# Linear attention: another order of instructions on TensorE, VectorE and ScalarE, both function-table loads moved, and the query's positive part taken by ScalarE

## The reference

```python
x = x + 0.5 * _L0_ffn_ref(_layernorm(x), ...)      # routed attention
x = x + _L0_attn_ref(_layernorm(x), ...)           # causal softmax attention
x = x + 0.5 * _L0_ffn_ref(_layernorm(x), ...)
x = x + 0.5 * _L1_ffn_ref(_layernorm(x), ...)      # 8 experts, top 2
x = x + _L1_attn_ref(_layernorm(x), ...)           # this one
x = x + 0.5 * _L1_ffn_ref(_layernorm(x), ...)

def _L1_attn_ref(x, Wq, Wk, Wv, Wp, bp, conv_w, conv_b):
    q, k, v = split_heads(x @ Wq.T), split_heads(x @ Wk.T), split_heads(x @ Wv.T)   # 16 heads of 8
    q = jax.nn.elu(q) + 1.0
    k = jax.nn.elu(k) + 1.0
    kv_state = jnp.einsum('bhnd,bhne->bhde', k, v)
    k_state = k.sum(axis=2)
    attn_out = jnp.einsum('bhnd,bhde->bhne', q, kv_state)
    denom = jnp.maximum(jnp.einsum('bhnd,bhd->bhn', q, k_state), 1e-06)[..., None]
    attn_out = (attn_out / denom).transpose(0, 2, 1, 3).reshape(b, s, d)
    xp = jnp.pad(x, ((0, 0), (1, 1), (0, 0)))
    local = xp[:, :-2, :] * conv_w[:, 0] + xp[:, 1:-1, :] * conv_w[:, 1] + xp[:, 2:, :] * conv_w[:, 2] + conv_b
    return (attn_out + local) @ Wp.T + bp
```

## Time and profile before

| | |
|---|---|
| median of 3 runs | 766.7 us (765.39 to 770.39) |
| profiled execution | 768.21 us |
| its span, first to last instruction | 766.4 us |
| PE busy | 614.0 us (80%) |
| DVE busy | 448.3 us (59%) |
| ACT busy | 426.9 us (56%) |
| POOL busy | 306.1 us (40%) |
| chain that ended last | PE 50%, ACT 18%, DVE 17%, issue 8%, DMA 4%, POOL 3% |
| mean granted TensorE clock | 0.913 |

### The profile page before, as it was taken

One profiled execution on the slowest core, in us unless ns is written; L12 is line 12 of the kernel. 1 busy time (PEld: TensorE's weight loads), 2 busy tenths in 40 slices (PEclk: granted clock), 3 DMA queues, 4 the chain that ended last, 5 costly groups with the idle time before them and its releaser, 6 DMA issues.

```text
span 766.4 us, 13125 instructions
## 1 busy us (share of the span) xinstructions
PE 614.0 (80%) x4624; PEld 454.7 (59%) x4624; DVE 448.3 (59%) x1401; ACT 426.9 (56%) x806; POOL 306.1 (40%) x384
## 2 busy tenths in 40 slices
PE   6789886379999997079887599999559769999990
PEld 3667683122222223067687589999547658999990
DVE  7883959831123215984858555556469783555572
ACT  5664634579999997444635543434343563434440
POOL 1243443213232321234341567766340036777553
PEclk9789999759999999589998799999879968999995
DMA  8311000668200000002002686666220057666645
GB/s 325 122 66 48 1 2 0 206 197 288 83 2 1 1 2 1 0 16 98 2 2 48 178 264 225 187 221 192 94 68 0 2 145 274 183 224 188 214 125 171
DMA packets 36051, 85.60 MB, mean 112 GB/s; under 512 B 5072, under 2 KB 20048, under 8 KB 34960
## 3 DMA queue, kind: packets, MB, share of 16 engines
q1 hardware_dynamic: 30992, 74.42, 29.5%
q0 software_dynamic: 4992, 10.31, 4.7%
HBM read 67.90 MB, written 16.81 MB: 111 GB/s over the span
## 4 chain that ended last, share of the span: by engine, by line
PE 50%; ACT 18%; DVE 17%; issue 8%; DMA 4%; POOL 3%; SPq 0%; ACTq 0%; DVEq 0%; POOLq 0%
PE ps L2021 17%; ACT arena L1494 9%; PE ps L2033 8%; PE ps L1725 3%; PE ps L1821 2%; ACT Xn L1302 2%; PE ps L1934 2%; PE ps L1767 1%; PE ps L1776 1%; PE ps L1800 1%; DVE stats L666 1%; DMA arena<-in_wq 1%; PE ps L1911 1%; DMA arena<-yd 1%; PE ps L2008 1%
## 5 line engine op out<-in xcount | busy, mean ns | idle before, releaser
L2021 PE MATMUL ps<-arena 128*128 128x256 f32 (+1 forms) x736 | 147.2, 350 | 2.9 <-issue 1.3
L1547 ACT ACTIVATE arena<-ps,arena 128x256 f32<-128x256 f32 (+1 forms) x184 | 81.0, 441 | 122.0 <-issue 76.6
L1494 ACT ACTIVATE arena<-ps 128x1024 f32<-128x1024 f32 x144 | 132.5, 1339 | 2.2 <-PE ps L1911 1.8
L2021 PEld LDWEIGHTS ps<-arena 128*128 128x128 f32 x736 | 122.2, 191 | 17.9 <-issue 3.4
L1018 DVE SCALAR_TENSOR_TENSOR arena<-ps,arena 128x256 f32<-128x256 f32 (+1 forms) x184 | 81.4, 443 | 75.6 <-ACT arena L1547 73.8
L639 POOL DMA_INDIRECT yd<-arena,wqk x78 | 76.7, 983 | 60.4 <-DVE arena L1040 49.4
L603 POOL DMA_INDIRECT arena<-xs,wqk x78 | 75.7, 970 | 37.6 <-issue 14.6
L590 POOL TENSOR_SCALAR_AFFINE_SELECT arena<-arena 128x512 f32<-128x512 f32 x64 | 39.9, 636 | 106.3 <-ACT arena L1494 106.3
L1934 PE MATMUL ps<-arena 128*32 128x512 f32 (+3 forms) x768 | 79.5, 502 | 1.0
L2033 PE MATMUL ps<-arena 128*128 128x128 f32 x624 | 77.3, 276 | 0.0
L2033 PEld LDWEIGHTS ps<-arena 128*128 128x128 f32 x624 | 73.3, 192 | 0.4
(11 more groups left out here) (298 smaller groups left out, 1138.3 us busy)
## 6 DMA issues: line engine op xcount, KB each, us to landing
arena<-in_wall SPq DMA_DIRECT2D x46, 836.0 KB, 4.6
arena<-slots SPq DMA_DIRECT2D x2, 2048.0 KB, 7.8
arena<-scr_q SPq DMA_DIRECT2D x8, 512.0 KB, 6.6
arena<-scr_k SPq DMA_DIRECT2D x8, 512.0 KB, 7.7
arena<-yd SPq DMA_DIRECT2D x8, 512.0 KB, 5.5
xs<-Xn SPq DMA_DIRECT2D x8, 260.0 KB, 5.5
scr_q<-arena SPq DMA_DIRECT2D x4, 384.0 KB, 4.5
scr_k<-arena SPq DMA_DIRECT2D x4, 384.0 KB, 4.2
```

What stands on the lines that cost most here:

```text
L1494: nc.scalar.activation(Pa[:, n0:n0 + FILL, :], ps[:, bank:bank + FILL, :], ACT.Exp, scale=AD ** -0.5).then_inc(sem("exp", i), 1)
L1547: nc.scalar.activation(sl[:, k % 3, 0:rows], ps[:, k % 3, 0:rows], ACT.Silu, bias=raw[:, slot, EW_BA + f:EW_BA + f + 1]).then_inc(sem("sil ...
L2021: ins = mm(ps[:, bank, 0:rows], raw[:, slot, w + P * f:w + P * (f + 1)], xTt[:, j % 2, 0:rows], start=True, stop=True)
```

## The change

Five things are done:

- **ScalarE, tables.** The dummy activation that loads the table of exp moves from behind `transposed(2)` to behind the roots of the second batch, ahead of its normalised rows. A second one, for the square root, is added behind the query activations; the next step's own dummy activation for the square root then finds its table loaded. The number of table loads stays.
- **ScalarE, queries.** Beside exp of a query chunk ScalarE now also takes its positive part, into the two slots of r2, and signals `qexp` after that. It waits for `lk(3)` and `lk(4)` before the first two (r2 is shared with the keys), and for `lq(1)` and `lq(2)` before the others.
- **VectorE, queries.** `query_map` is one scalar_tensor_tensor on SBUF tiles, in place of a tensor_scalar and a scalar_tensor_tensor that reads PSUM.
- **VectorE, order.** `local(0)` stands ahead of the first `key_map`; `local(1)` behind the second one; two query maps stand ahead of the KV masks, two behind.
- **TensorE, order.** Two query chunks go ahead of the fourth key chunk. The convolution's products (`convolved`) no longer stand together behind `state`, but one by one between the query products, transposes and projections.

The diff, cut to its core:

```diff
-                key_map(0)
-                local(0)
-                key_map(1)
-                key_map(2)
-                local(1)
-                key_map(3)
-                for c in range(NC):
+                def query_map(c):
                     dve.wait_ge(*at("qexp", i, c + 1))
                     sl_ = slice(HALF * c, HALF * (c + 1))
-                    link(nc.vector.tensor_scalar(lE[:, sl_], lE[:, sl_], 1.0, None, ALU.min))
-                    nc.vector.scalar_tensor_tensor(out=lqT[:, sl_], in0=ps[:, c, :], scalar=0.0, in1=lE[:, sl_],
-                                                   op0=ALU.max, op1=ALU.add).then_inc(sem("lq", i), 1)
-
+                    nc.vector.scalar_tensor_tensor(out=lqT[:, sl_], in0=lE[:, sl_], scalar=1.0,
+                                                   in1=r2_[:, c % 2].rearrange("p t d -> p (t d)"), op0=ALU.min, op1=ALU.add
+                                                   ).then_inc(sem("lq", i), 1)
+
+                local(0)
+                key_map(0)
+                key_map(1)
+                local(1)
+                key_map(2)
+                key_map(3)
+                query_map(0)
+                query_map(1)
                 for b in range(B):
                     dve.wait_ge(*at("state", i, b + 1))
...
+                query_map(2)
+                query_map(3)
...
                 def normal_batch(b):
                     roots(i, b)
+                    if b == B - 1:
+                        preload(ACT.Exp)
                     act.wait_ge(*at("offset", i, b + 1))
...
                 transposed(i, 2)
-                preload(ACT.Exp)
                 keys_values(0)
...
                     act.wait_ge(*at("lqp", i, c + 1))
-                    nc.scalar.activation(lE[:, HALF * c:HALF * (c + 1)], ps[:, c, :], ACT.Exp
+                    nc.scalar.activation(lE[:, HALF * c:HALF * (c + 1)], ps[:, c, :], ACT.Exp)
+                    if c < 2:
+                        act.wait_ge(*at("lk", i, c + 3))
+                    else:
+                        act.wait_ge(*at("lq", i, c - 1))
+                    nc.scalar.activation(r2_[:, c % 2].rearrange("p t d -> p (t d)"), ps[:, c, :], ACT.Relu
                                          ).then_inc(sem("qexp", i), 1)
+                preload(ACT.Sqrt)
...
+                transpose_chunk(i, 0)
+                for c in range(3):
+                    transpose_chunk(i, c + 1)
+                    key_value(c)
+                query(0)
+                query(1)
+                key_value(3)
+                query(2)
+                query(3)
+                pe.wait_ge(*at("ones_bias", i, 1))
+                pe.wait_ge(*at("krelu", i, NC))
+                state(0)
+                state(1)
+                attended(0)
+                attended(1)
+                convolved(0)
+                turned_back(0)
+                convolved(1)
+                turned_back(1)
+                attended(2)
+                projected(0)
+                attended(3)
+                projected(1)
+                turned_back(2)
+                convolved(2)
+                turned_back(3)
+                projected(2)
+                convolved(3)
+                projected(3)
```

More of the change, by code:

```diff
@@ L2050, in lin, with key_value, query, state @@
                 pe.wait_ge(sem("smallw_in"), 48)
[L2051 to L2058, removed]
+                def key_value(c):
+                    pe.wait_ge(*at("xT", i, c + 1))
+                    if c >= 2:
+                        pe.wait_ge(*at("krelu", i, c - 1))
                     for t in range(4):
-                        ins = mm(four(c - 1, 4)[:, t, :], XT[:, P * (4 * c - 4 + t):P * (4 * c - 3 + t)],
+                        ins = mm(four(c, 4)[:, t, :], XT[:, P * (4 * c + t):P * (4 * c + t + 1)],
                                  linc[:, LC_WKV:LC_WKV + 2 * D], start=True, stop=True)
                     ins.then_inc(sem("lkvp", i), 1)
-                for c in range(NC):
+                def query(c):
                     mm(ps[:, c, :], linc[:, LC_WQ:LC_WQ + D], XT[:, HALF * c:HALF * (c + 1)], start=True, stop=True
                        ).then_inc(sem("lqp", i), 1)
-                pe.wait_ge(*at("ones_bias", i, 1))
-                pe.wait_ge(*at("krelu", i, NC))
-                for b in range(B):
+                def state(b):
                     for j in range(TB):
@@ L2074, in lin, with attended, convolved @@
                     ins.then_inc(sem("state", i), 1)
-                pe.wait_ge(*at("local", i, B))
-                for c in range(NC):
+                def attended(c):
+                    pe.wait_ge(*at("KV", i, 1 if c == 0 else 2))
                     pe.wait_ge(*at("lq", i, c + 1))
+                    if c >= 2:
+                        pe.wait_ge(*at("AT", i, c - 1))
+                    for t in range(4):
+                        ins = mm(numer(c)[:, t // 2, t % 2, :], lqT[:, P * (4 * c + t):P * (4 * c + t + 1)], KV[:, c // 2, :],
+                                 start=True, stop=True)
+                    ins.then_inc(sem("num", i), 1)
+                def convolved(c):
+                    pe.wait_ge(*at("local", i, c // 2 + 1))
+                    pe.wait_ge(*at("qexp", i, c + 1))
                     for t in range(4):
```

## The result

Over 14 runs each the changed kernel takes 765.7 us in the median (761.47 to 770.24) and the kernel before 768.18 (764.85 to 771.92). The ratio is **0.9942, with a 95% interval of 0.9921 to 0.9964**: 4.5 us less, between 2.8 and 6.1. The medians lie only 2.5 apart. The forecast was 2.8 less and a median of 763.9 us. The median came 1.8 above that, and the size forecast lies at the edge of the interval. With such scatter the runs alone do not say whether the gain is 2.5 or 4.5.

The account below looks back on a forecast made before the run. The prediction took TensorE's unbroken chain from 574.88 to 591.4 us, then alternating engines with TensorE holes, as the bound. The load's gain nearly lost to the collision, TensorE's order won 2.8: median 766.7 - 2.8 = 763.9 us, range 761.2 to 766.6.

Parts of the forecast that it names:

- Part 1: ScalarE's exp table load moved ahead of the normalised rows: rows 0.33 later, TensorE's third key chunk 1.2 us earlier.
- Rival 3: ScalarE's table load is longer in its new place, drain 1.3 us more: gain 2.4, 764.3 us, chance 0.05.
- Part 2: VectorE's local(0) collides with GpSimd's add: lk(1) 2.4 us later, nearly all of the table load's gain lost.
- rival 1: No collision, GpSimd's add does not hold up VectorE's local(0): gain 3.8, 762.9 us, chance 0.17 with partial collision.
- Rivals 1 and 2: No collision; or GpSimd first or its add stretched, gain 2.3 to about 0.5, up to 766.2 us, chance 0.10.
- Part 3: Query maps on ScalarE and VectorE: query products start at 586.45 against 590.36, after a 0.5 us wait for KV.
- Part 4: TensorE's new order: 15.3 us without a hole from 586.45, ending at 601.7 against 604.48, 2.8 us won.
- Part 5: Stage's end: VectorE's last add 3.8 us earlier, but TensorE's transposes and gates stand last and move only 2.8.
- Rival 4: Granted clock falls inside the stage: up to 5.5 us lost, 769.4 us; chance 0.06, including a later clock return.

Follow-up runs that it names:

- Trials 2 and 3: Changed kernel with the exp table load back behind the third transpose's copy, without and with GpSimd's add late: ratios to the kernel before 0.9967 and 0.9937.
- Trial 1: Changed kernel with GpSimd's bias add also waiting for the last query map, run twice: ratios to the kernel before 0.9924 and 0.9937.
- trial 5: Changed kernel with TensorE's old order behind state (four convolution pieces, then query products and the old loop): ratio to the kernel before 0.9947.
- trial 6: Kernel before with TensorE's new order alone: ratio to the kernel before 0.9979.
- trial 9: Kernel before with GpSimd's bias add moved behind the last query map: ratio to the kernel before 1.0045.
- trial 7: Kernel before with TensorE's new order alone, plus 14 idle products ahead of the query products: ratio to the kernel before 0.9971.

## Why the prediction was right, and where its size came short

- **Part 1** (load in a gap of 1.08, 0.33 too long): as forecast, 1.40 from the load's begin to the rows. The Trainium skill (page "ScalarE: Activation LUTs", section "What ACT_TABLE_LOAD costs") puts a switch at 2.66 us; the trace does not agree, with its 1.40. Trials 2 and 3 show the 1.2 us, and that the collision eats it. Rival 3 is out.
- **Part 2** (collision): the two L1067 took 6.75 (6.9 forecast), the add 5.27 (over 5), `key_map(0)` ended at 12.97 on the stage clock (12.8 forecast, 0.33 of clock not counted). Which yields, which no row of before could tell, is settled: the first L1067 ran its 1.29 untouched, and the add, begun beside it, took 0.74 longer than alone. The Trainium skill (page "SBUF — State Buffer", section "Who interferes with whom") lets the one that issues first keep the shared ports for its whole instruction; the trace agrees. Trial 1 gives the price, 1.25 at the last add; rival 1 had put it at 1.0. Rivals 1 and 2 are out.
- **Part 3**: TensorE idle 0.99 before state (0.9) and 0.44 before the query products (0.5); first division 22.05 (22.2).
- **Part 4 is the step that failed in size.** "A chunk of query products, convolution or projection costs 1.06 (4.24 / 4)": it costs 0.89 to 0.99. From the first query product to the next step's transposes TensorE took 13.4 us (588.63 to 602.06), not 15.3. I had read 4.24 us without a hole as TensorE's own pace, while each piece waited for a query map of VectorE, in holes shorter than a matmul's record; trial 5 gives 3.57 for the same work. Of the 1.9 us, 1.3 are these twelve pieces; the rest is the four transposes, put at 0.6 by the length of a record where the next work starts 0.43 to 0.49 behind. The 1.9 us missing from the forecast are the difference between 2.8 and the 4.7 of the stage. The view of before that gave the 4.24 spoke against both prices: it has 1.00 for a chunk of query products (590.36) and, further on, 0.89 for a chunk of projections and 0.45 for a transpose:

```profile
595.69 0.89 PE ps L2092 x8
596.58 0.45 PE ps L2086 x4
```

- **Part 5** fell with it: with TensorE 1.9 faster, VectorE's adds, not the gates, ended last, as they had before the change.
- Rival 4 did not show in the stage; the clock stood at 1.00 until the gates were done. It had called the cost of a low clock to the gates little; trial 1 shows 0.91 us on sixteen of their products (2.82 against 1.91).
- The gain is no sum of its parts: TensorE's order alone 1.35 at best, the positive part alone 0.95, all but TensorE's tail 1.17, together 4.69. TensorE's order alone waits 3.61 us for KV (trial 6), 0.44 in the change; VectorE's work alone meets TensorE's old tail with its holes (trial 5).

What stays open: why executions of one kernel spread by 5 us and more outside this stage; that part was not tried. No trial takes back alone the place of the KV masks between the query maps, the two query chunks ahead of the fourth key chunk, or the load of the square root's table, so what each of these is worth is not shown.

## What to carry to other kernels

A row of matmuls that the trace shows as busy without a hole can still be paced by another engine: compare the starts, piece by piece, with the signals that it waits for, and with other rows of the same work, before its length is taken as a price. Before an instruction moves, look at what GpSimd does in its new place: an instruction of VectorE that reads SBUF there may stand still for nearly the whole length of GpSimd's (4.39 of 4.50 us in trial 9). And an edit whose price is nothing in one order (the table load) may be worth its full length in another.

## What the runs showed of the hardware that I had not expected

- A tensor_scalar of 128x16 with one SBUF input, 0.22 us elsewhere, stood still 4.39 us beside GpSimd's add (trial 9); the divisions from PSUM beside the same add kept their 0.76.
- After a hole of 3.61 us TensorE's granted clock stood at 0.50 (1.2 GHz) for the next work, which took 1.4 us longer (trial 6). With idle products in the hole it stayed at 1.00 (trial 7), but so it did over an empty hole of 3.54 us (trial 9): one execution each, so the idle products are not shown to be the cause.
- In both executions of trial 1 the clock fell while TensorE was busy with gate products of 8 columns (0.63 in 604 to 606 us). This cost 0.9 us at the gates' end, and left 0.7 of the 1.25 won at the next step's first routing instruction. It fell among the gate products of the kernel before, too.
